# A gate's products moved from TensorE to VectorE in six blocks of a fused graph layer and mixture-of-experts kernel

## The reference

```python
x = x + L0_gnn(layernorm(x), adj)   # two graph layers: (A^T (h W_in + b)) W_out + h W_self, layernorm, relu
x = x + L0_ffn(layernorm(x))        # 8 experts, one per row
x = x + adj @ (layernorm(x) * W)
x = x + L1_ffn(layernorm(x))        # experts chosen by segment of 64 rows
```

```python
logits = layernorm(x) @ gate_w + gate_b          # gate_w is 128 x 8
idx = argmax(softmax(logits)); prb = its value
pos = position of the row among the rows of its expert; rows past a capacity of 640 are dropped
```

## Time and profile before

| what | value |
|---|---|
| median of 3 runs | 995.26 us |
| the profiled execution | 995.61 us |
| its span | 993.8 us |
| TensorE (PE) matmul busy | 969.9 us, 98% |
| VectorE (DVE) busy | 508.8 us, 51% |
| ScalarE (ACT) busy | 318.7 us, 32% |
| GpSimd (POOL) busy | 188.2 us, 19% |
| chain that ended last, on PE | 88% of the span |
| second layer's products, L1792 x512 | 226.7 us, no idle time before them |
| steps 1 to 7, 343.52 to 549.00 us | PE busy 204.8 of 205.5 us, DVE 84.0, POOL 42.2; DMA share 0.83, 318 GB/s |

### The profile page before, as it was taken

How to read it: one execution, slowest core, us unless ns; L and a number is a source line. 1 busy time by engine, 2 the same in 40 slices (tenths; PEclk the granted TensorE clock), 3 DMA queues, 4 the chain that set the end, 5 groups by cost and what they waited for, 6 DMA issues and landing times.

```text
span 993.8 us, 15482 instructions
## 1 busy us (share of the span) xinstructions
PE 969.9 (98%) x4894; PEld 560.7 (56%) x4894; DVE 508.8 (51%) x1487; ACT 318.7 (32%) x628; POOL 188.2 (19%) x216
## 2 busy tenths in 40 slices
PE   7999999999999999999999899989999999999997
PEld 4555555555555544444444378844566666666665
DVE  6333133133133234444334478657867867867854
ACT  3554564564560110000000145315142242341332
POOL 3201100101101121222221326544102201102101
PEclk8999999999999999999999899999999999999999
DMA  9994873573502598878878258626999998999841
GB/s 350 423 371 174 355 327 126 224 330 128 219 1 85 228 355 310 328 295 321 303 296 331 107 162 280 231 85 237 405 351 325 344 333 327 356 330 331 297 138 54
DMA packets 64478, 262.72 MB, mean 264 GB/s; under 512 B 8836, under 2 KB 24904, under 8 KB 52102
## 3 DMA queue, kind: packets, MB, share of 16 engines
q1 hardware_dynamic: 61254, 257.16, 69.0%
q0 software_dynamic: 2864, 4.39, 1.3%
q10 hardware_dynamic: 272, 0.13, 0.0%
HBM read 243.85 MB, written 20.01 MB: 265 GB/s over the span
## 4 chain that ended last, share of the span: by engine, by line
PE 88%; DVE 4%; DVEq 2%; issue 2%; ACT 2%; DMA 1%; POOL 1%; ACTq 0%; SPq 0%; POOLq 0%
PE PA L1812 22%; PE PA L1792 22%; PE PA L2049 15%; PE O L1987 3%; PE O L2153 3%; PE O L1861 3%; PE O L1833 1%; PE T L2162 1%; PE SM L2153 1%; PE SR L2153 1%; PE PA L1770 1%; PE O L1823 1%; PE O L2130 1%; ACT U L779 1%; PE PA L1977 1%
## 5 line engine op out<-in xcount | busy, mean ns | idle before, releaser
L1812 PE MATMUL PA<-ring,S 128*128 128x512 f32 x512 | 232.8, 601 | 2.8 <-DMA ring<-in_adj_cols 2.8
L1792 PE MATMUL PA<-ring,U 128*128 128x512 f32 x512 | 226.7, 595 | 0.0
L1812 PEld LDWEIGHTS PA<-ring,S 128*128 128x128 f32 x512 | 96.5, 192 | 105.9 <-issue 104.1
L1792 PEld LDWEIGHTS PA<-ring,U 128*128 128x128 f32 x512 | 94.8, 190 | 106.6 <-issue 106.5
L2050 PE MATMUL PA<-ring 128*64 128x256 f32 x560 | 130.8, 380 | 0.0
L699 ACT ACTIVATE work<-ring 128x2048 int8<-128x2048 f32 x64 | 122.3, 1910 | 8.9 <-issue 4.7
L2049 PE MATMUL PA<-ring,S 128*64 128x256 f32 x448 | 105.2, 380 | 0.3 <-DVE ring L1628 0.3
L2049 PE MATMUL PA<-ring 128*64 128x256 f32 x336 | 81.2, 381 | 0.0
L2049 PEld LDWEIGHTS PA<-ring,S 128*64 128x64 f32 x448 | 60.5, 137 | 35.4 <-issue 6.2
L2050 PEld LDWEIGHTS PA<-ring 128*64 128x64 f32 x560 | 75.5, 137 | 0.0
L2049 PEld LDWEIGHTS PA<-ring 128*64 128x64 f32 x336 | 44.9, 137 | 24.3 <-issue 2.3
(11 more groups left out here) (300 smaller groups left out, 1370.3 us busy)
## 6 DMA issues: line engine op xcount, KB each, us to landing
ring<-in_adj_cols SPq DMA_DIRECT2D x52, 2048.0 KB, 8.5
ring<-in_adjT_cols SPq DMA_DIRECT2D x32, 2048.0 KB, 9.3
ring<-w_d SPq DMA_DIRECT2D x128, 256.0 KB, 3.8
ring<-in_adj_cols SPq DMA_DIRECT2D x8, 1024.0 KB, 13.0
ring<-in_Wr SPq DMA_DIRECT2D x4, 2048.0 KB, 9.1
w_d<-ring SPq DMA_DIRECT2D x8, 1024.0 KB
work<-in_w SPq DMA_DIRECT2D x16, 256.0 KB
disp_d<-U SPq DMA_DIRECT2D x4, 650.0 KB, 19.6
```

Of the source, the lines that this page charges most:

```text
L1792: mm = nc.tensor.matmul(out_T[:, :], X[:, t * D:(t + 1) * D], ring[slot][t // HT][:, (t % HT) * BW:(t % HT + 1) * BW], start=n == 0, stop= ...
L1812: mm = nc.tensor.matmul(PA[k % 2][:, :], S[:, t * D:(t + 1) * D], ring[slot][t // HT][:, (t % HT) * BW:(t % HT + 1) * BW], start=t == 0, s ...
```

## The change

For blocks 1 to 6 (`BY_ROWS`) the gate's products of the rows are made by VectorE. The gate's weights, turned (8 rows of 128 numbers) and repeated on all partitions, are loaded once as `gate_rows`, 512 KB, in `tail_inputs`. `gate_products` multiplies, for each of the 4 tiles of rows, x1 (repeated) by 4 of the gate's rows at a time, 128x512, and reduces each product over its 128 numbers: 8 multiplies and 8 reduces a block, into `lg`, with a drain after each pair. It stands in route after the statistics and ahead of the wait for the second power. In these blocks tail_b, ScalarE's copy and tail_c are gone, and tail_d moves from product 25 to product 31. Blocks 7 and 8 keep the old order; the counts of their semaphores are adapted (`turned_before`).

```diff
-        WORK = 22 * 256 + 64
+        WORK = 24 * 256 + 88
...
+        gate_rows = part(at, E1 * D)
+        at += E1 * D
+        gate_part = [part(at, BW), hnT]
+        assert at + BW <= WORK
+        BY_ROWS = range(1, NB - 1)
...
+        def turned_before(k):
+            return len([i for i in range(1, k) if i not in BY_ROWS])
...
                 sp.dma_start(gbc, A["gate_b_bc"]).then_inc(s_wts2, 16)
+                sp.dma_start(gate_rows, A["gate_rows"]).then_inc(s_wts2, 16)
                 sp.dma_start(w_s, A["WsT"]).then_inc(s_wself, 16)
...
-                act.wait_ge(s_hn2p, k)
-                nc.scalar.copy(hnT, T[1][:, :]).then_inc(s_hn2T, 1)
+                if k not in BY_ROWS:
+                    act.wait_ge(s_hn2p, turned_before(k) + 1)
+                    nc.scalar.copy(hnT, T[1][:, :]).then_inc(s_hn2T, 1)
...
+            def gate_products(x1):
+
+                half = E1 // 2
+                for t in range(BT):
+                    for h in range(2):
+                        nc.vector.tensor_tensor(tiles(gate_part[h], half), x1[t].unsqueeze(1).to_broadcast([P, half, D]),
+                                                tiles(gate_rows[:, h * half * D:(h + 1) * half * D], half), ALU.mult)
+                    dve.drain()
+                    for h in range(2):
+                        at = t * E1 + h * half
+                        nc.vector.tensor_reduce(lg[:, at:at + half], tiles(gate_part[h], half), AX.X, ALU.add)
+                    dve.drain()
+
...
                 dve.drain()
+                if k in BY_ROWS:
+                    gate_products(x1)
                 lnorm_scale(k, 1)
...
-                dve.wait_ge(s_lg, k)
-                alone(dve)
-                nc.vector.tensor_tensor(e3(lg), e3(SR[:, 0:BT * E1]), bce(rstd[:, 0:BT]), ALU.mult)
+                if k in BY_ROWS:
+                    nc.vector.tensor_tensor(e3(lg), e3(lg), bce(rstd[:, 0:BT]), ALU.mult)
+                else:
+                    dve.wait_ge(s_lg, turned_before(k) + 1)
+                    alone(dve)
+                    nc.vector.tensor_tensor(e3(lg), e3(SR[:, 0:BT * E1]), bce(rstd[:, 0:BT]), ALU.mult)
...
-            dve.wait_ge(s_wts2, 48)
+            dve.wait_ge(s_wts2, 64)
...
-                pe.wait_ge(s_hn2T, k)
+                pe.wait_ge(s_hn2T, turned_before(k) + 1)
...
                 tail_a(k)
+                if k in BY_ROWS:
+                    products(U, sl, 2, 31, s_quart2, ROWS2, slot)
+                    tail_d(k)
+                    products(U, sl, 31, NT, s_quart2, ROWS2, slot).then_inc(s_agg2, 1)
+                    return
                 products(U, sl, 2, 16, s_quart2, ROWS2, slot)
...
+        "gate_rows": bc(_np.ascontiguousarray(g["L0_ffn_gate_w"].T)),
```

More of the change, by code:

```diff
@@ L164, in build @@
         rb4 = part(at, 4)
-        assert at + 4 <= WORK
+        at += 4
+        gate_rows = part(at, E1 * D)
[3 more added lines that the diff above has]
+        BY_ROWS = range(1, NB - 1)
         at = 0
```

## The result

The kernel after takes 999.7 us in the median, the kernel before 997.1 us beside it (20 runs each; the ratio is 1.0029, interval 1.0018 to 1.0040). In a later measurement the same change gave 1.0056 (1.0037 to 1.0075). So it is slower, by about 3 us in the first measurement and 5 to 6 us in the second, where +2.6 us was forecast. At the bound of 0.3% this lies between "the same", to which I gave 0.49, and "slower", 0.44; the range held it.

What follows compares the result with a forecast made beforehand. TensorE alone was taken to set the pace; step 1's stall (5.2 us late after step 2) outweighed 4 x 0.66 us returned by later blocks, +2.6 us, so the median went from 995.26 to 997.8 us, range 993.8 to 1003.0.

Steps and rivals of the forecast that it cites:

- The gain: TensorE, blocks 1 to 6: bound by TensorE alone, a block takes 28.12 us, 1.33 less, 8.0 us for six.
- The added work: VectorE, each changed block: 16 instructions take 11.04 us; tail_d can start 16.34 us after the statistics start.
- Rival 2: VectorE's products are short, 9.76 us a block: 993.9 us, or 991.4 without the clock's fall; chance 0.12.
- rival 4: VectorE's products are long, 12.3 us a block: 1005 us; chance 0.10.
- Step 1: TensorE waits 5.4 us at tail_d, since late transfers, 1.33 us later through the 512 KB load, delay VectorE's statistics.
- S(1): Start of step 1's statistics on VectorE, forecast at T + 14.35, T being the start of tail_a's turn.
- The clock: TensorE, step 1: its wait halves the clock for 5 us after work resumes, losing 2.5 us.
- Rival 1: The clock doesn't fall in step 1: +0.7, 996.0 us; chance 0.15.
- Steps 3 to 6: GpSimd's power, behind four scatters issued after tail_d (start: tau), is 1.00 us late; TensorE waits 0.67, blocks 28.79 us.
- S at T + 8.66: VectorE's statistics start 8.66 us after tail_a's turn, read from step 3 before the change, used for step 2.
- Rival 5: The change is inert, every saved microsecond waited out at tail_d: 995.3 us; chance 0.03.
- Rival 3: GpSimd, steps 3 to 6: one of four scatters held by VectorE's multiplies, 1.6 us more a step, 1004.2 us; chance 0.15.

Runs made afterwards that it cites:

- masksplit: The kernel after with masklater and split together, the later stage's 512 KB weight load left where it was; 0.9906 of the kernel before.
- masklater: The kernel after with the waits for the next block's quarters and thresholds and the previous block's scatters moved behind VectorE's products; 0.9987 of the kernel before.
- latews: The kernel after with the later stage's 512 KB weight loaded one turn later; 1.0024 of the kernel before.
- warm: The kernel after with six dummy products on TensorE between product 31 and tail_d in step 1; 1.0038 of the kernel before.
- after_again: The kernel after, unchanged, measured again in a later series; 1.0056 of the kernel before.
- only1: The kernel after with VectorE's products in block 1 alone, blocks 2 to 8 as in the kernel before; 1.0081 of the kernel before.
- split: The kernel after with GpSimd issuing three scatters, then add_branch's power, then the fourth scatter; 1.0111 of the kernel before.
- both: The kernel after with masklater, split and latews together; 0.9926 of the kernel before.
- from2: The kernel after with VectorE's products in blocks 2 to 6 only, the load of the gate's rows unmoved; 0.9991 of the kernel before.

## Why the prediction was right, and where it was off

**The gain.** TensorE alone needs 28.12 us a block: exact, in step 2 of the kernel after and in masksplit. Off TensorE's list of work, 8 us were really there; masksplit gets 7.5 of them.

**The added work.** 11.04 us predicted, 10.99 measured. From S to tail_d 16.34 predicted; 373.11 - 356.88 = 16.23 in step 1, 16.26 in step 3. Rival 2 (short products) and rival 4 (long ones) are excluded by this.

**Step 1.** S(1) was to be at T + 14.35 and was at T + 14.83; the wait 5.4 and 5.57 (5.73 by the prediction's reckoning). The cause is shown by the thresholds' row in the chain and by masklater (same work, other place, no wait). That the load has a share is shown by latews; its size, 1.33 us in the prediction, only to between 0.9 and 2.5 us.

**The clock.** I took 2.5 us, and warm shows 2.6. Rival 1 (it doesn't fall) is excluded. That the size fits is partly luck: the clock was at half for 6.8 us in all in step 1 of the kernel after, after_again and latews, but for 3.4 us in only1 and in split's step 3, where the six entries lost only 1.6 us; which of the two comes isn't explained by these runs. The prediction also misread one row: a mean of 0.79 from 674 to 675 puts the clock's return at about 674.4, not 674.8, 5.9 us after work resumed. The 5 us that it took doesn't depend on that.

**Steps 3 to 6: the term that was mis-sized.** "TensorE waits 0.67 us" was 1.03, 0.76, 1.55 and 0.72 as printed, and 1.20, 0.92, 1.71 and 0.88 by the prediction's reckoning; four blocks were 117.23 us, not 115.16, and these 2.1 us are most of the miss of T(8) - T(1) (+5.1, not +2.6). The mechanism, the power queued behind four scatters, is shown by split's x1 and by masksplit. Four things made it larger. The scatters started 406.72 - 403.81 = 2.91 us after tau, not 2.50, since VectorE's last steps for the weights (L1380 to L1386) used to hide before tail_d and now stand between it and `idx`. The fourth scatter took up to 0.08 us longer than in the earlier trace rows. Against that the power started at once behind it, where I had put 0.2 us between them; together it started at T + 5.05 to T + 5.11 in steps 3, 4 and 6, not at T + 4.78, and x1 followed it. In step 3 S also waited for the scatters' landing, which I hadn't priced: VectorE's row there is

```profile
416.86 0.87 DVE L1021 BATCH_NORM_STATS2 st<-S 128x6 f32<-128x128 f32 x4 [1.96 <-DMA disp_d<-work]
```

with 0.3 us more than mask2's bare 1.67. The fourth thing is step 5's further 0.8 us. Two rows of VectorE, which the other steps don't have, make it up:

```profile
462.98 0.19 DVE L1385 TENSOR_REDUCE work<-work 128x4 f32<-128x32 f32 x1 [0.44 <-issue]
...
490.59 0.19 DVE L1369 TENSOR_REDUCE work<-work 128x4 f32<-128x32 f32 x1 [0.45 <-issue]
```

In step 3 these instructions start 0.26 and 0.27 us after the one before them, here 0.63 and 0.65. The first pause, behind step 4's tail_d, delays `idx`, the scatters and step 5's power (T + 5.49); the second stands between the products and L1378, so that L1350 to L1378 takes 3.56 us and not 3.18. Together they are 0.75 us. after_again, warm, latews, masklater and split have both pauses at the same two instructions, and both and masksplit have them too, where step 5 lasts 28.50 and 28.31 us. In from2, whose instructions before them differ, they stand elsewhere (484.63 and 512.38), and there it is step 6 that has the further 0.8 us and not step 5. What holds VectorE in them isn't shown; the profile names no engine or transfer.

S at T + 8.66 was one step's number besides: in the kernel before, steps 2 and 4 had T + 9.23 and T + 9.63 (2.24 and 2.63 us in front of S, not 1.67). In the kernel after, where x1 comes later, this cost nothing in steps 4 to 6: their S waited 1.67 to 1.69 us.

**Rival 5** (the change is inert) is excluded by T(8) - T(1), 5.1 us longer, and by blocks of 28.11 to 36.43 us.

**Rival 3** (scatters held by VectorE's multiplies of two SBUF tensors) didn't come: the fourth scatter was 1.05 us at most, not 2.58. The contention that the Trainium skill names ("GPSIMD Engine Reference", section "Key points") is at most 0.08 us a scatter here, where the multiplies are 128 wide.

## What to carry to other kernels

When work moves from the engine that sets the pace to an idle one, price the chain that it lengthens, not the idle engine's free time: draw each step's deadlines, then put the added work in front of the longest wait for a transfer, where it is free, and not behind it. Then look at every queue whose work the move pushes past the step's end; here one in-order queue with four scatters ahead of a small power cost a microsecond a block. Two waits can cover each other, so an edit that is bad alone (split, 1.0111 where the kernel after has 1.0056 beside it) can be the missing half of a good one (masksplit, 0.9906).

## What the runs showed that I had not expected

Scatters of 128 rows of 520 bytes, each 1 us of GpSimd's time, were seen landed at very different times. In split S starts 6.3 us after the end of the fourth one's issue in step 3, 5.0 in step 5, but 3.0 and 2.8 in steps 2 and 4, with the scatter as its releaser in all four. All transfers together moved 316 to 331 GB/s during the long ones and 266 to 272 during the short; that this is the cause isn't shown.

A wait of TensorE of 3.53 us was followed by the half clock (split, step 3), one of 4.82 us in only1 cost no more (1.6 us on six entries), and one of 2.38 us cost no clock (split, step 5).

VectorE's products seem to hold GpSimd in one place. The power for route takes 1.01 us in the kernel after, where it starts 0.06 or 0.07 us ahead of the first product. In steps 1 to 6 of masklater, masksplit and both it starts 0.01 to 0.03 us behind the product's start and takes 1.54 to 1.58 us. The two go together in every trace, though no run changed this alone. Nobody waits for the power there, so it costs nothing.
